# Six of a destination tile's 13 product chunks of layer 1 issued between the groups of the next tile's aggregation, with the bf16 copy of the counts ahead of the copy of the transposed sums

## What is computed

```python
# layer 0
t1 = feat @ W1
msg = (t1[src] + feat[src] * feat[dst] @ W2) / (sqrt(out_deg[src]) * sqrt(out_deg[dst]))[:, None]
embed = where(in_cnt > 0, t1 + segment_sum(msg, dst), 0) + b
embed = leaky_relu(embed, 0.01);  embed = embed / max(norm(embed), 1e-12)
# layer 1
norm = dinv[row] * ew * dinv[col]
h7 = segment_sum((h @ W)[col] * norm[:, None], row) + b
out = relu(h7 @ W1 + b1) @ W2 + b2
```

## Time and profile before

| | us |
|---|---|
| median of 3 runs | 2332.73 (2323.42 to 2341.97) |
| the profiled execution | 2324.01 |
| its span in the trace | 2322.1 |
| PE / DVE / ACT / POOL busy | 1936.2 / 1340.0 / 487.8 / 1082.0 |
| granted TensorE clock, mean (1.0 = 2.4 GHz) | 0.896 |

### The profile page before, as it was taken

One profiled execution on the slowest core, in us unless ns is written; L12 is line 12 of the kernel. 1 busy time (PEld: TensorE's weight loads), 2 busy tenths in 40 slices (PEclk: granted clock), 3 DMA queues, 4 the chain that ended last, 5 costly groups with the idle time before them and its releaser, 6 DMA issues. The chain is left out here.

```text
span 2322.1 us, 23042 instructions
## 1 busy us (share of the span) xinstructions
PE 1936.2 (83%) x7229; PEld 1169.0 (50%) x7239; DVE 1340.0 (58%) x1970; ACT 487.8 (21%) x636; POOL 1082.0 (47%) x1561
## 2 busy tenths in 40 slices
PE   5499587767777767667669999999989999999996
PEld 1188422254544444445446776677874344434443
DVE  7977598823323322223224555566568777878885
ACT  1000200033333223223325545330043000000000
POOL 1888888887888888888886000000004000000000
PEclk9755588988988888889889999999999999999998
DMA  7888830035334535433444775238724555655663
GB/s 275 333 326 325 323 125 16 1 97 186 116 114 169 172 114 175 151 128 134 150 150 169 258 253 189 80 103 309 226 68 123 158 163 164 186 168 153 171 180 105
DMA packets 338570, 394.92 MB, mean 170 GB/s; under 512 B 114000, under 2 KB 319674, under 8 KB 325563
## 3 DMA queue, kind: packets, MB, share of 16 engines
q1 hardware_dynamic: 219593, 306.93, 38.4%
q10 hardware_dynamic: 93110, 86.22, 11.2%
q0 software_dynamic: 25792, 0.88, 0.9%
HBM read 221.43 MB, written 172.51 MB: 170 GB/s over the span
## 5 line engine op out<-in xcount | busy, mean ns | idle before, releaser
L377 POOL DMA_INDIRECT table<-valT,idxT x806 | 809.7, 1005 | 158.9 <-issue 157.6
L2005 PE MATMUL psum<-wgt,big 128*65 128x384 f32 (+3 forms) x1600 | 530.1, 493 | 1.0 <-DVE wgt L1953 1.0
L1953 DVE SCALAR_TENSOR_TENSOR wgt<-ratio,l3q,fcj 128x768 f32<-128x768 f32 (+2 forms) x400 | 412.1, 1046 | 94.6 <-PE psum L2005 86.4
L789 PE MATMUL psum<-hx,region 128*128 128x257 f32 x1250 | 336.5, 417 | 123.8 <-issue 65.0
L2005 PEld LDWEIGHTS psum<-wgt,big 128*65 128x65 f32 x1600 | 219.7, 138 | 302.8 <-issue 298.7
L789 PEld LDWEIGHTS psum<-hx,region 128*128 128x128 f32 x1250 | 247.2, 208 | 179.2 <-issue 77.9
L789 PE MATMUL psum<-region,g 128*128 128x512 f32 (+1 forms) x672 | 305.6, 599 | 16.2 <-DVE big L592 13.4
L592 DVE TENSOR_TENSOR big<-big,psum 128x512 f32<-128x512 f32 (+1 forms) x325 | 210.4, 665 | 148.2 <-PE psum L789 125.0
L375 POOL MEMSET rest<- 128x256 f32 x722 | 237.0, 328 | 48.7 <-issue 48.0
L1000 POOL PARTITION_ALL_REDUCE edges<-edge x1 | 0.5, 517 | 495.2 <-DVEq L1369 495.2
L789 PEld LDWEIGHTS psum<-region,g 128*128 128x128 f32 x672 | 129.9, 206 | 154.7 <-issue 109.8
(11 more groups left out here) (218 smaller groups left out, 1671.6 us busy)
## 6 DMA issues: line engine op xcount, KB each, us to landing
table<-tk SPq DMA_DIRECT2D x25, 3200.0 KB
fcj<-counts SPq DMA_DIRECT2D x150, 384.0 KB, 3.5
tk<-table SPq DMA_DIRECT2D x25, 1664.0 KB
counts<-region ACTq DMA_DIRECT2D x25, 1600.0 KB
tk<-table SPq DMA_DIRECT2D x25, 1536.0 KB
fcj<-counts SPq DMA_DIRECT2D x50, 448.0 KB, 3.7
counts_t<-region ACTq DMA_DIRECT2D x25, 800.0 KB
counts_b<-region ACTq DMA_DIRECT2D x25, 800.0 KB
```

Of the source, the lines that this page charges most:

```text
L377: eng.indirect_dma_start(out=table, out_offset=bass.IndirectOffsetOnAxis(idxT[:, c:c + 1], 0), in_=valT[:, c, :], in_offset=None).then_inc ...
L789: mm = lambda o, l, r_, st, sp: eng.matmul(o, l, r_, start=st, stop=sp, skip_group_check=True)
L1953: eng.scalar_tensor_tensor(out=wgt[:, n % NW, u, 0:w], in0=rb[:, 2 * i + u, t0 * P:t0 * P + w], scalar=qs[:, k, 2 * i + u:2 * i + u + 1], ...
L2005: last = eng.matmul(acc[p % 2][u][0:FW, b, 0:hi - lo], ftx[:, k, 2 * i + u, :], wgt[:, n % NW, u, lo:hi], start=k == 0, stop=k == NT - 1, ...
```

## The change

The constant `EARLY = 6` is new. On TensorE chunks 0 to 5 of `prev` are now issued in pairs behind groups 3, 4 and 5 of `cur`'s aggregation; chunks 6 to 8 stand behind g = 6, then `turn_ab`, chunks 9 and 10, `dense`, chunks 11 and 12. VectorE lifts chunks 0 to 5 before it waits for `q`. ScalarE makes `wt` ahead of `take` 3, and makes and stores `cb` ahead of `abT`.

```diff
+EARLY = 6
 # VectorE
                 if prev and cur:
                     eng.wait_ge(sem("wt"), prev[0] + 3)
                     itself(row(wt, prev[0]))
+                    for n in range(EARLY):
+                        lift(n)
...
-                    for n in range(5 if last else 13):
+                    for n in range(EARLY if cur else 0, EARLY + 2 if last else 13):
                         lift(n)
...
-                    fill(5, 6)
+                    fill(8, 9)
...
-                    fill(7, 8)
+                    fill(10)
...
-                    fill(9, 10, 11, 12)
+                    fill(11, 12)
 # ScalarE
                 if prev:
                     normal(prev[0], g1)
-                take(k, 3)
-                take(k, 4)
-                if prev:
                     eng.wait_ge(sem("ag"), 13 * prev[0] + 1)
                     eng.activation(wt, tk[:, prev[1], :, :, 1], ACT.Copy).then_inc(sem("wt"), 1)
-                take(k, 5)
-                take(k, 6)
+                for g in range(3, 7):
+                    take(k, g)
...
-                eng.wait_ge(sem("abt"), k + 1)
-                eng.activation(abT[:, :, :].rearrange("p c n -> p (c n)"), pab, ACT.Copy).then_inc(sem("abfree"), 1)
                 if prev:
                     eng.wait_ge(sem("cb_out"), 16 * k)
                 eng.activation(cb, cs, ACT.Copy).then_inc(sem("cb"), 1)
...
                 eng.dma_start(counts_b[bass.ds(k, 1), :, :, :].rearrange("a p j d -> (a p) j d"), cb).then_inc(sem("cb_out"), 16)
+                eng.wait_ge(sem("abt"), k + 1)
+                eng.activation(abT[:, :, :].rearrange("p c n -> p (c n)"), pab, ACT.Copy).then_inc(sem("abfree"), 1)
 # TensorE
                         if g + 3 < 7:
                             turn(k, s, g + 3)
+                        if prev and g in (3, 4, 5):
+                            if g == 3:
+                                eng.wait_ge(sem("g1"), prev[0] + 1)
+                                eng.wait_ge(sem("diag"), prev[0] + 1)
+                            gathered(range(2 * g - 6, 2 * g - 4))
                     mul.then_inc(sem("q"), 1)
...
                 if prev:
-                    gathered(range(0, 3))
+                    gathered(range(EARLY, EARLY + 3))
                 turn_ab()
                 if prev:
-                    gathered(range(3, 5))
+                    gathered(range(EARLY + 3, EARLY + 5))
                 dense()
                 if prev:
-                    gathered(range(5, 13))
+                    gathered(range(EARLY + 5, 13))
```

More of the change, by code:

```diff
@@ L860, in step, with gathered @@
             def step(cur, prev, last=False):
+                def gathered(chunks):
+                    j, z = prev
+                    of, g = (wt, g1) if cur else (tk[:, 0, :, :, 1], hk)
+                    for n in chunks:
+                        eng.wait_ge(sem("af"), 13 * j + max(n + 1, 3))
+                        if n < 12:
+                            mul = mm(pL[:, n % 3, :], g[:, n % 2 * P:n % 2 * P + P], of[:, 4 * (n // 2):4 * (n // 2) + 4, :], True, True)
+                        else:
+                            for o in range(2):
+                                mul = mm(pL[:, 0, o * P:o * P + P], g[:, o * P:o * P + P], of[:, NT - 1, :], True, True)
+                        mul.then_inc(sem("ag"), 1)
                 if cur:
@@ L873, in step @@
                             turn(k, s, g + 3)
-                    mul.then_inc(sem("q"), 1)
[L876 to L886, removed]
+                        if prev and g in (3, 4, 5):
[3 more added lines that the diff above has]
+                            gathered(range(2 * g - 6, 2 * g - 4))
+                    mul.then_inc(sem("q"), 1)
                 def turn_ab():
@@ L898, in dense @@
                     mul.then_inc(sem("e"), 1)
-                if prev:
+                if not cur:
                     eng.wait_ge(sem("g1"), prev[0] + 1)
                     eng.wait_ge(sem("diag"), prev[0] + 1)
-                if not cur:
                     gathered(range(13))
```

## The result

The changed kernel takes 2356.95 us (median of 12 runs, 2348.20 to 2368.63), the kernel before 2333.74 in 12 runs of the same chip: a ratio of 1.0103 with a 95% interval of 1.0081 to 1.0125. So the change costs 23 us where the prediction said 15. The profiled executions took 2351.88 and 2324.01 us, 27.9 apart, and the two traces show where the difference lies.

What follows compares the result with a forecast made beforehand. Bound: late PE signals while POOL scatters, then TensorE without a gap. First stage -0.6 us a tile, but costlier second-stage tiles, gave +11.8; ends +3.5 made +15.3: 2348 us against the median 2332.7, range 2296 to 2380.

Steps and rivals of the forecast that it cites:

- The chunks in the scatter stage: First stage, chunks 0 to 5 between groups 3 to 6: net -1.5 us in each of 13 late periods.
- d: Change in us a tile of the first stage: -0.6, the mean of 13 periods at -1.5 and 4 at +2.2.
- the prediction's own formula: Whole kernel's change in us: (24 - 757.4 / (44.55 + d)) x 29.4 - 187.2 + 3.5.
- the second stage alone decides: Rival: first stage gains nothing, +22 us, 2355, +8 if store held; no gain or a loss there: 0.35 together.
- 17.1 to 17.8 tiles by 1247: Check on the first stage: tiles done by 1247 us, instead of 17 periods, as the scatter's end is fixed.
- `wt` ahead of take 3: ScalarE's copy delays group 3 on PE: +2.0 us a tile in the second stage, +2.2 in 4 prompt first-stage tiles.
- The store of `cb`: Second stage, `dense` waits for `abT` behind the store: +0.6 us a tile, between 0 and 1.8; first stage nothing.
- ends: First `q` with a tile before it +5.15 us once, final products about -1.6: +3.5 in all.
- gaps filled in full: Rival: first-stage gaps of PE behind groups 3 to 5 filled, -5.15 us a tile, -43 us, 2290; chance 0.15.
- the clock as well: Rival: PE's clock in the first stage also recovers, -7 us a tile, -71 us, 2262; chance 0.05.
- Lateness grows: Rival: more PE signals lengthen first-stage waits, +2 us a tile, +44 us, 2377; no gain or a loss there: 0.35 together.
- signals are late only while POOL scatters: First stage: what PE tells others arrives 6 to 9 us late, in about 14 of 18 tiles.

Runs made afterwards that it cites:

- b_wt: The kernel before with ScalarE's takes 3 and 4 put behind the copy `wt`, nothing else changed: 2316.50 us to 2302.71, 1.0043.
- a_three: The changed kernel with EARLY = 3, one chunk instead of two behind each of groups 3, 4 and 5: 2386.82 us to 2327.16 of the kernel before, 1.0227.
- a_abt: The changed kernel with ScalarE's copy `abT` again ahead of `cb` and its store: 2313.05 us, 1.0033 to the kernel before.
- a_short: The changed kernel with GpSimd's scatter making only the first 34 of 103 groups of transfers: 2108.87 us in one run.
- c_g5: The kernel before with chunks 0 to 2 behind group 5, ScalarE's order as before: 2332.59 us to 2327.16, 1.0011.
- b_short: The kernel before with GpSimd's scatter making only the first 34 of 103 groups of transfers: 2011.57 us in one run.
- b_pause: The kernel before with three more memsets on GpSimd at the start of each group of 8 transfers, from column 280 on: 2272.09 us to 2327.16, 0.9763.
- b_win: The kernel before with three more GpSimd memsets per group of transfers, for columns 280 to 489 only: 2231.27 us to 2203.41, 1.0124.
- b_rests: The kernel before with, from column 280, four memsets at each group's head and none between its transfers: 2462.00 us to 2308.60, 1.0645.

## Why the prediction was right in its sign and short by a third

*The chunks in the scatter stage:* right in the mechanism, and a little too hopeful. The chunks fill the gaps behind group 3, and chunk 3 waits for chunk 0's addition, as the step said. The forecast d was -0.6 us a tile; apart from the first period the trace has 723.0 us in 16 periods after 723.1 before, d = 0. The term that was mis-sized is the lateness: 7 us were taken for chunk 0's signal, and the tile shown has 10.6, with a second wait of 3.29 us ahead of chunk 5 that the step left out. With d = 0 the prediction's own formula gives +22, and its rival "the second stage alone decides" said 2355, with +8 for the held store. The result, 2357, is nearest to that rival, but in part by luck: with the 30.3 us that a late period really takes, the formula gives +28 at d = 0, as the two traces have it, and +21 at d = -0.6. The medians' difference, 23 us with an interval of 19 to 29, allows both. That d is 0 rests on one trace of each kernel.

*A slip in the sum:* of the four prompt waits for `q` the first, at 489.6 us, opens the stage and belongs to none of the 17 periods. With 3 prompt tiles and 14 late ones d is -0.85 and the sum is +12 instead of +15, further from the measured +23.

*"17.1 to 17.8 tiles by 1247":* wrong, 16.9.

*`wt` ahead of take 3:* right in place, releaser and size; forecast +2.0 a tile. The wait is 1.8 us in both kernels, and alone it makes a tile 2.1 us longer (b_wt).

*The store of `cb`:* right that it is partly covered: 0.8 us a tile, taken at 0.6 between 0 and 1.8. The open question, whether the store's issue is held, is settled: in the changed kernel's second stage it is held in all seven tiles, for 4.2 to 6.7 us, until 7.7 to 10.2 us after the issue of `counts_t`, where the prediction took 10.4 if held. PE reached `dense` first in five of them. Two tiles that follow each other, the first of them without a wait of PE (ScalarE's timeline):

```profile
1373.31 4.18 ACTq L775 DMA_DIRECT2D counts_b<-region  x1
1377.54 0.60 ACT L777 ACTIVATE abT<-psum 128x512 f32<-128x512 f32 x1 [4.46 <-PE psum L896]
1402.11 5.68 ACTq L775 DMA_DIRECT2D counts_b<-region  x1
```

In a_three, whose fewer early chunks cover less of it, PE's wait is 3.4 to 4.0 us, with the half clock behind it.

*The term that was missing:* PE's longer busy time beside the new waits. The sum let PE run as before behind them. In the second stage its busy time grew by 6.4 us, 0.9 a tile (193.4 to 186.9). 3.4 us of it are the half clock in two of seven tiles; in a_abt it takes four tiles and 6.7 us, in a_short 16 of 24 tiles and 27 us. The other 3.0 us stand beside the 2.6 of b_wt, at full clock. The prediction weighed the clock only as something to be won back in the first stage. The two waits themselves were forecast at 7 x 2.6 = 18.2 us and measured at 12.6 + 5.6 = 18.2. So the profiled difference, 12.6 us above the sum (27.9 to 15.3), is 6.4 of longer busy time and 6.8 that the first stage was to give back (7 - 6.77 periods of 29.4 us) and did not; ends and rounding are the rest. That the two waits came out equal in sum is luck: the one was 0.2 us a tile shorter than forecast, the other as much longer. The Trainium skill (TensorE: Matmul & The Clock Gate, on oscillation) has the clock fall after idle stretches and rise after busy ones. By that rule, the trace agrees in a_abt's four long periods; b_wt, where waits of up to 1.93 us cost no clock, shows that the length of the wait alone does not tell.

*The rivals:* "gaps filled in full" and "the clock as well" did not hold, and c_g5 shows why for the smallest case: the wait moves behind the moved work. "Lateness grows" held in part: late waits grew in sum (523 to 599 us), but the stage did not get longer. The reading under all of this, that signals are late only while POOL scatters, is borne out by b_short and by every second stage here; that they are always late while it scatters is not so (b_pause, b_win).

*What stays open:* whether the store's place also costs in the first stage (after to before 1.0103, a_abt 1.0033, their second stages 3.1 us apart, but on different chips and with first stages that vary by 5 us and more); what in the scatter holds PE's signals (that the spacing of its transfers matters is shown, the path is not, nor why nothing is late in b_win's later part); when a wait brings the half clock; and why chips differ. The gaps of 1.17 us are only coincidences in time; b_pause is the test of them.

## What to carry to other kernels

Before filling a gap, ask what the filling work itself must signal: if the gap is made of late signals, products that end with another one only move the wait. Price a copy that is moved ahead of what feeds a saturated TensorE by how much later the feed then comes, in every stage without slack, and allow for the half clock behind the new wait; here a copy of 3.1 us made a wait of 1.8, which cost 2.1 us a tile at full clock (b_wt) and 3.1 where the half clock came in four of seven tiles (a_abt). And look for the cause of the gaps outside the engine that has them: three more memsets per group on GpSimd were worth 55 us on one chip, more than any order of TensorE's work tried here, and cost 67 on another, so such a cure has to be timed on more than one.

## What the runs showed of the hardware

- While GpSimd scatters with an indirect transfer every 1.45 us, what PE tells ScalarE and VectorE starts them 7.6 to 10.6 us after the end of PE's record in the tiles shown; with the scatter cut short no such wait is left (b_short). A rest of 1.1 us more per group of 8 transfers takes it away (b_pause: 13 periods at clock 1.00); with 1.27 us between the transfers of a group and the rests gathered at its head the waits grow to 21.8 us (b_rests). Transfers every 1.45 us are not enough by themselves: in b_win, behind its rests, nothing is late from 850 to 1240 us.
- One and the same kernel takes 2203 to 2334 us on different chips, the pausing one 2270 and 2272.
- A wait of 1.6 to 1.9 us in an otherwise gapless stream of products is sometimes followed by the half clock and sometimes not: in none of seven in b_wt, in two of seven in the changed kernel, in four of seven in a_abt and in 16 of 24 in a_short, where it costs 1.7 us each. A wait of 3.4 to 4.0 us ahead of `dense` was followed by it in seven of seven (a_three).
- The issue of a 0.8 MB store on ScalarE's queue can hold that engine. Where it comes 3.5 us behind the store of `counts_t`, it is held for 4.2 to 6.7 us in the seven tiles of the changed kernel's second stage and for 2.1 to 6.5 us in 6 of the 17 of its first; where it comes 11 us behind it, in none of a_abt's seven (0.34 us). What it waits for the traces don't show.
